# Later rope products and earlier up chunks in the score phase of a fused transformer layer

## The chip, the core and the metric

One core of one Trainium2 chip runs the whole layer in one launch. The metric is device microseconds of that core.

## The reference

The layer takes x of shape (4, 256, 256): 4 batches of 256 tokens, width 256.

```python
x = x + attn(layernorm(x)); x = x + ffn(layernorm(x))
# attn: q, k, v = h @ Wq.T, h @ Wk.T, h @ Wv.T ; rope over the full width on q and k
#   16 heads of 16; k_feat, q_feat = elu(k) + 1, elu(q) + 1
#   mem_out = (q_feat @ (k_feat.T @ v)) / (q_feat @ k_feat.sum)     # linear attention
#   attn = softmax(q @ k.T / 4) @ v
#   out = (g * mem_out + (1 - g) * attn) @ Wo.T,  g = sigmoid(gate) per head
# ffn: hidden = silu(x @ W1.T) * (x @ W3.T)     # 1024 wide
#   out = fwht(hidden) @ W2.T                   # Walsh-Hadamard transform, normalised
```

## The kernel before, in words

All engines are programmed by hand: each has its own list of instructions, run in order, and they meet at semaphores. Nothing is planned by a compiler, so the place of a call in an engine's list is its place in that engine's queue.

A product that needs full precision is made of three fp32r matmuls: each operand is split in a high part (rounded, written by ACT) and a low part (the rest, written by DVE or POOL). The Hadamard transform is multiplied into W2 at the start, in round 0.

The work runs in rounds. Round r holds the attention of batch r, the projections of batch r+1 and the feed-forward part of batch r-1, with the last chunk (7) of batch r-2. It has these phases:

- The score phase, heads h = 0 to 15. PE computes the scores of head h+2 (a pair of matmuls, L978) into one of two score banks; DVE reduces them to row maxima (L698), and PE can only write a bank again when DVE has read it. In the same loop PE does the residual and output projection of batch r-1 (L1056, L1065), the q and k projection of batch r+1 (`project_qk`), the transposes of the second LayerNorm's rows (L938), up unit 0 and 1 of chunk 7 of batch r-2 (at h = 5 and 6), the v projection of batch r+1 (`project_v`, at h = 8 and 9) and the up units of chunks 0 to 2 of batch r-1 (`UP_AT`, at h = 10 to 15). A chunk is 128 of the 1024 hidden columns; it has two up units (W1 and W3), each six matmuls (L1087, L1091). DVE does, beside the row maxima, the LayerNorm (`ln_statistics`, `ln_normalise` L681), the four rope products of batch r+1 (`rope_product` L709, at h = 3 to 6), `low_h2T` (L690, at h = 7) and the gates (`ffn_gate` L806, L809) of chunk 7 (h = 6) and chunk 0 (h = 12).
- The bridge. PE transposes the maxima (`transpose_max` L988), reads the linear memory (`read_memory` L1046), does chunk 3's up units and the down products (`ffn_down` L1109, L1113) of chunks 0 and 1. ACT (`split_max` L373) and DVE (`low_max`) write the negated maxima, and DMAs put them in rows of q_stack.
- The exp phase, heads 0 to 15. PE computes the shifted scores (`shifted_scores` L996), ACT takes their exponent (L384), and PE multiplies by v (`product_v` L1013); chunks 4 to 6 and the down products of chunks 2 to 6 lie in between.

The banks matter at three places. `project_v` of batches 1 to 3 writes misc_bank0, which batch r+1's second q and k projection (c = 1) has written before, so for batches 2 and 3 it waits for the fourth rope product; for batch 1 the q and k projections lie in exp banks. Chunk 2 uses the same bank as chunk 0 and waits for chunk 0's gate (`hid_s`). `read_memory` writes misc_bank0 again, so it waits for `evac_v` (L348).

ACT in the score phase: the second residual's copy (L398), tanh of chunk 7 (L413), h2T_hi (L404), the high parts of the roped q and k (`split_parts` L340, two), hid_hi of chunk 7 (`split_hid` L419), `evac_v`, then `ffn_step` of chunks 0 and 1, and `split_max`. `ffn_step(n)` is tanh of chunk n and hid_hi of chunk n-1.

POOL in a round: the reciprocal root of the LayerNorm (`ln_power` L551, called rstd below), two rope sums (L558), hid_lo of chunk 7 (`hid_low` L577), the low parts of the roped q and k (L565, two), in round 1 alone the low part of W2 (L617, tile w_lo), the negative part for elu (L569), hid_lo of chunks 0, 1 and the others. PE's down product of a chunk ends with matmuls on hid_lo (L1113). ACT's tanh of chunk n waits for hid_lo of chunk n-3.

SP loads the stacks of batch r+1: it waits for exp head 8 (or 16) of batch r, writes zeros, then copies part_hi and part_lo. Each wait is one in a fixed order.

Of the kernel before, what the change touches and what calls it, by code (L numbers as in the profile page):

```python
# [88 lines left out]
def build(nc, x, wqT, wkT, wvT, woT, gate, w1T, w3T, w2T, const, out):  # L89
    with ExitStack() as ctx:  # L90
# [112 lines left out]
        def chunk(b, c):  # L203

            return FC * b + c if 0 <= b < NB else None
# [17 lines left out]
        def has(b):  # L223
            return 0 <= b < NB
# [93 lines left out]
        def _(act):  # L318
# [81 lines left out]
            def evac_h2T(b):  # L400
                act.wait_ge(h2T_ps, b + 1)
                if b >= 1:
                    act.wait_ge(up_ps, FC * b)
                act.activation(h2T_hi[:], pv_bank[:], ACT.Copy).then_inc(h2T_hi_s, 1)  # L404
# [74 lines left out]
            for r in range(NB):  # L479
                if has(r - 1):  # L480
                    evac_x2(r - 1)
                if has(r - 2):
                    ffn_tanh(chunk(r - 2, 7))
                if has(r - 1):
                    evac_h2T(r - 1)
                if has(r + 1):
                    split_parts(r + 1, 0)
                if has(r - 2):
                    split_hid(chunk(r - 2, 7))
                if has(r + 1):  # L490
                    split_parts(r + 1, 1)
                if r >= 1 and has(r + 1):
                    evac_v(r + 1)
                ffn_step(chunk(r - 1, 0))
                ffn_step(chunk(r - 1, 1))
                if has(r):
                    split_max(r)
                ffn_step(chunk(r - 1, 2))
                if has(r):
                    evac_lin(r, 0)  # L500
                    evac_lin(r, 1)
                ffn_step(chunk(r - 1, 3))
                for h in range(NH):
                    if has(r):
                        exp_head(r, h)
                    if h in (2, 6, 12):
                        ffn_step(exp_chunk(r, {2: 4, 6: 5, 12: 6}[h]))
                    if h == 12 and r == NB - 1:
                        split_hid(chunk(r - 1, 5))
                    if h == 5 and has(r + 1):  # L510
                        exp_elu(r + 1)
                    if h == 8 and has(r + 2):
                        evac_hT(r + 2)
                    if h == 11 and has(r):
                        evac_att(r, 0)
                    if h == 15 and exp_chunk(r, 6) is not None:
                        split_hid(chunk(r - 1, 6))
                if has(r):
                    evac_att(r, 1)
                if has(r + 1):  # L520
                    evac_kfT(r + 1)
                if has(r):
                    evac_att(r, 2)
                if r == 0:
                    split_w2()
# [14 lines left out]
        def _(pool):  # L540
# [64 lines left out]
            for r in range(NB):  # L605
                if has(r - 1):
                    ln_power(LN[(2, r - 1)])
                if has(r + 1):
                    rope_sums(r + 1, 0)
                if has(r + 1):  # L610
                    rope_sums(r + 1, 1)
                hid_low(chunk(r - 2, 7))
                if has(r + 1):
                    low_parts(r + 1)
                if r == 1:
                    pool.wait_ge(w2_hi_s, 1)
                    pool.tensor_tensor(w2_lo[:], w2_b, w2_hi[:].bitcast(F32), ALU.subtract).then_inc(w2_lo_s, 1)  # L617
                if r == 0:
                    butterfly(pool, 0)
                    ln_power(LN[(1, 2)])  # L620
                if has(r + 1):
                    negative_part(r + 1)
                if r == 0:
                    butterfly(pool, 1)
                hid_low(chunk(r - 1, 0))
                hid_low(chunk(r - 1, 1))
                for c in range(2, FC - 1):
                    hid_low(exp_chunk(r, c))
                    if c == 3 and r > 0 and has(r + 2):
                        ln_power(LN[(1, r + 2)])  # L630
                    if c == 4 and has(r):
                        norm_linear(r)
# [8 lines left out]
        def _(dve):  # L641
# [205 lines left out]
            for r in range(NB):  # L847
                for h in range(NH):
                    if h == 0 and has(r - 1):
                        combine(r - 1, NP - 1)  # L850
                    if has(r) and h < NH - 2:
                        row_maxima(r, (h + 2,))
                    if h == 2 and has(r - 1):
                        ln_statistics(LN[(2, r - 1)])
                    if h == 12 and r == 0:
                        memory_strips(0)
                    if 3 <= h < 7 and has(r + 1):
                        rope_product(r + 1, h - 3)
                    if h == 3 and has(r - 1):
                        ln_normalise(LN[(2, r - 1)])  # L860
                    if h == 6:
                        ffn_gate(chunk(r - 2, 7))
                    if h == 7 and has(r - 1):
                        low_h2T(r - 1)
                    if h == 12:
                        ffn_gate(chunk(r - 1, 0))
                if r == 0:
                    ln_statistics(LN[(1, 2)])
                if has(r):
                    low_max(r)  # L870
                if r == 0:
                    gate_weights()
                ffn_gate(chunk(r - 1, 1))
                ffn_gate(chunk(r - 1, 2))
                if has(r - 2):
                    second_residual(r - 2)
                if r > 0 and has(r + 2):
                    ln_statistics(LN[(1, r + 2)])
                ffn_gate(chunk(r - 1, 3))
                if has(r + 2):  # L880
                    ln_normalise(LN[(1, r + 2)])
                ffn_gate(chunk(r - 1, 4))
                if has(r):
                    weights(r, 0)
                if has(r + 1):
                    features(r + 1)
                ffn_gate(chunk(r - 1, 5))
                if has(r + 2):
                    low_hT(r + 2)
                ffn_gate(exp_chunk(r, 6))  # L890
                if has(r):
                    combine(r, 0)
                if has(r + 1):
                    row_maxima(r + 1, (0,))
                if has(r):
                    combine(r, 1)
                if has(r + 1):
                    row_maxima(r + 1, (1,))
                    memory_strips(r + 1)
# [14 lines left out]
        def _(pe):  # L914
# [219 lines left out]
                free[bank.name] = (had_sb, u + 1)  # L1134


            UP_AT = ((),) * 10 + ((0,), (1,), (2,), (3,), (4,), (5,))

            UP_IN_EXP = {0: (4, 0), 1: (4, 1), 3: (5, 0), 4: (5, 1), 8: (6, 0), 11: (6, 1)}
            DOWN_IN_EXP = {2: 2, 7: 3, 12: 4}  # L1140
# [25 lines left out]
            for r in range(NB):  # L1166


                for h in range(NH):
                    if has(r) and h < NH - 2:  # L1170
                        scores(r, (h + 2,))
                    if h == 0 and has(r - 1):
                        residual_in(r - 1)
                    if h in (1, 2) and has(r - 1):
                        project_out(r - 1, h - 1)
                    if has(r + 1):
                        if h in (0, 1) or h in (2, 3) and r == 0:
                            project_qk(r + 1, h)
                        if h in (3, 4) and r >= 1:
                            project_qk(r + 1, h - 1)  # L1180
                    if r == 0 and h in (4, 5):
                        project_v(1, h - 4)
                    if r == 0 and h in (6, 7):
                        hadamard(2, h - 6, True)
                    if r == 0 and 8 <= h < 12:
                        hadamard(3, h % 2, h >= 10)
                    if h == 8 and r == 0:
                        transpose_features(0)
                    if h == 11 and r == 0:
                        memory(0)  # L1190
                    if h == 6 and has(r - 1):
                        transpose_rows(LN[(2, r - 1)])
                    if h in (5, 6):
                        ffn_up(chunk(r - 2, 7), h - 5)
                    if h in (8, 9) and r >= 1 and has(r + 1):
                        project_v(r + 1, h - 8)
                    if h == 9:
                        ffn_down(chunk(r - 2, 7))
                    for i in UP_AT[h]:
                        ffn_up(chunk(r - 1, i // 2), i % 2)  # L1200
# [84 lines left out]
```

## Time and profile before

| what | value |
|---|---|
| median of 3 runs | 217.6 us (216.65 to 218.44) |
| profiled execution | 218.47 us, span 216.7 us |
| granted TensorE clock | mean 0.976 |
| PE busy | 193.2 us (89%) |
| DVE busy | 148.2 us (68%) |
| ACT busy | 99.2 us (46%) |
| POOL busy | 92.0 us (42%) |

The span runs from the first to the last instruction of the profiled execution. Busy shares are means over all phases; the phases differ. In the rows of a timeline the times are the start and the duration, and the bracket tells how long the engine was idle before and what ended the wait. Rows of several equal instructions are merged ("x2"), their duration is then that of all of them. On PE two matmuls overlap, so one of 0.28 us is followed by the next after 0.12.

### The profile page before, as it was taken

How to read it: one execution, taken by the hardware profiler on the slowest of the kernel's cores; microseconds unless marked ns; L12 is line 12 of the kernel's file. 1: busy time of each engine (PE TensorE's matmuls, PEld its weight loads, DVE VectorE, ACT ScalarE, POOL GpSimd, SP SyncE). 2: the span in 40 equal slices, each digit the busy share in tenths (PEclk: the TensorE clock that was granted, in tenths of full speed). 3: DMA queues.
4: the chain of work that ended last, by engine and by line, in shares of the span. 5: the costliest groups of instructions: out<-in, count | busy, mean ns of one | idle time of the engine just before them, and what ended most of it. 6: DMA issues, size and time to landing. Idle time of an engine off the chain costs nothing.

```text
span 216.7 us, 4078 instructions
## 1 busy us (share of the span) xinstructions
PE 193.2 (89%) x1476; PEld 164.2 (76%) x1476; DVE 148.2 (68%) x329; ACT 99.2 (46%) x199; POOL 92.0 (42%) x84
## 2 busy tenths in 40 slices
PE   7898898499995998999979999996689988979993
PEld 3396797347794997878968998785589966869993
DVE  6499898963899963569898636299796345754442
ACT  3356715287722344884024368840215677231330
POOL 7719999990003895342039521320112231030332
PEclk9999999957999999999999999999999999997999
DMA  6998620003430000053100000533000100001001
GB/s 179 356 371 186 188 70 0 9 0 80 116 105 0 2 9 0 0 153 99 53 0 0 3 8 0 148 91 110 0 3 6 48 3 2 0 3 48 0 3 48
DMA packets 12639, 13.54 MB, mean 62 GB/s; under 512 B 1388, under 2 KB 11852, under 8 KB 12620
## 3 DMA queue, kind: packets, MB, share of 16 engines
q1 hardware_dynamic: 11148, 11.96, 18.6%
q10 hardware_dynamic: 1472, 1.32, 2.2%
q8 instruction: 12, 0.20, 0.4%
q14 instruction: 7, 0.06, 0.1%
HBM read 5.71 MB, written 1.05 MB: 31 GB/s over the span
## 4 chain that ended last, share of the span: by engine, by line
issue 38%; PE 27%; POOL 23%; DVE 7%; ACT 2%; POOLq 1%; DVEq 0%; ACTq 0%
PE exp_bank L1087 5%; POOL hid_lo L577 5%; PE score_bank L1144 4%; POOL w_lo L603 4%; PE score_bank L1087 3%; POOL prod L569 3%; PE exp_bank L1091 3%; PE down_bank L1109 2%; POOL narrow_raw L584 2%; POOL w_lo L596 2%; DVE prod L709 2%; POOL w_lo L617 2%; DVE rowmax_pad L698 2%; POOL part_lo L565 2%; PE score_bank L1091 2%
## 5 line engine op out<-in xcount | busy, mean ns | idle before, releaser
L577 POOL TENSOR_TENSOR hid_lo<-wide_raw,hid_hi 128x256 fp32r<-128x256 f32 x32 | 23.9, 747 | 71.4 <-ACT hid_hi L419 71.4
L698 DVE TENSOR_REDUCE rowmax_pad<-score_bank 128x2 f32<-128x512 f32 x64 | 42.8, 681 | 4.3 <-PE score_bank L978 4.2
L384 ACT ACTIVATE prob<-exp_bank 128x512 f32<-128x512 f32 x64 | 37.0, 601 | 17.2 <-PE exp_bank L996 16.7
L978 PE MATMUL score_bank<-k_stack,q_stack 128*128 128x256 f32 x128 | 27.3, 303 | 8.6 <-DVE rowmax_pad L698 8.5
L996 PE MATMUL exp_bank<-q_stack,k_stack 128*128 128x256 f32 x128 | 27.6, 318 | 4.1 <-DMA q_stack<-nmT_lo 2.3
L996 PEld LDWEIGHTS exp_bank<-q_stack,k_stack 128*128 128x128 f32 x128 | 19.9, 203 | 11.7 <-ACT prob L384 6.7
L978 PEld LDWEIGHTS score_bank<-k_stack,q_stack 128*128 128x128 f32 x128 | 19.3, 189 | 12.2 <-DVE rowmax_pad L698 8.3
L551 POOL TENSOR_TENSOR rstd<-var_eps,mhalf 128x2 f32<-128x2 f32 x8 | 5.6, 704 | 37.5 <-DVE var_eps L671 37.5
L806 DVE SCALAR_TENSOR_TENSOR wide_raw<-wide_raw,score_bank 128x256 f32<-128x256 f32 x16 | 6.7, 417 | 20.0 <-ACT wide_raw L413 20.0
L413 ACT ACTIVATE wide_raw<-exp_bank 128x256 f32<-128x256 f32 x16 | 6.1, 384 | 29.1 <-PE exp_bank L1091 27.1
L1087 PE MATMUL exp_bank<-h2T_hi,w_hi 128*128 128x256 f32 x64 | 17.8, 300 | 0.7 <-ACT h2T_hi L404 0.7
L1109 PE MATMUL down_bank<-w_hi,hid_hi 128*128 128x256 f32 x64 | 17.3, 293 | 0.0
L1087 PE MATMUL score_bank<-h2T_hi,w_hi 128*128 128x256 f32 x64 | 17.1, 291 | 0.0
L1087 PE MATMUL exp_bank<-h2T_hi,w_lo 128*128 128x256 f32 x64 | 16.9, 286 | 0.0
L1109 PE MATMUL down_bank<-w_lo,hid_hi 128*128 128x256 f32 x64 | 16.7, 283 | 0.0
L1087 PE MATMUL score_bank<-h2T_hi,w_lo 128*128 128x256 f32 x64 | 16.4, 280 | 0.0
L419 ACT ACTIVATE hid_hi<-wide_raw 128x256 fp32r<-128x256 f32 x32 | 13.3, 417 | 3.4 <-DVE wide_raw L809 3.1
L1113 PE MATMUL down_bank<-w_hi,hid_lo 128*128 128x256 f32 x64 | 13.1, 286 | 1.0 <-POOL hid_lo L577 0.9
L1013 PE MATMUL pv_bank<-prob,v_strips 128*32 128x256 f32 x192 | 13.7, 406 | 0.1
L1087 PEld LDWEIGHTS exp_bank<-h2T_hi,w_hi 128*128 128x128 f32 x64 | 12.6, 197 | 1.3 <-ACT h2T_hi L404 0.9
L1091 PE MATMUL exp_bank<-h2T_lo,w_hi 128*128 128x256 f32 x64 | 13.1, 286 | 0.0
L1087 PEld LDWEIGHTS exp_bank<-h2T_hi,w_lo 128*128 128x128 f32 x64 | 12.7, 198 | 0.0
(142 smaller groups left out, 483.2 us busy)
## 6 DMA issues: line engine op xcount, KB each, us to landing
q_stack<-part_hi SPq DMA_DIRECT2D x16, 128.0 KB
k_stack<-part_hi SPq DMA_DIRECT2D x14, 128.0 KB
xs<-in_x SPq DMA_DIRECT2D x4, 256.0 KB, 3.2
prob<-in_w2T SPq DMA_DIRECT2D x1, 1024.0 KB, 9.4
wide_raw<-in_w1T SPq DMA_DIRECT2D x1, 1024.0 KB, 11.4
wide_raw<-in_w3T SPq DMA_DIRECT2D x1, 1024.0 KB, 12.8
q_stack<-part_lo SPq DMA_DIRECT2D x8, 128.0 KB
k_stack<-part_lo SPq DMA_DIRECT2D x7, 128.0 KB
```

Source lines behind the costliest of these rows:

```text
L384: act.activation(prob[:, h % 8], exp_bank[h % 2][:], ACT.Exp, scale=SCALE).then_inc(prob_s, 1)
L419: act.activation(hid_hi[:, n % 3, :], ffn_work[n % 3], ACT.Copy).then_inc(hid_hi_s, 1)
L577: pool.tensor_tensor(hid_lo[:, n % 3, :], ffn_work[n % 3], hid_hi[:, n % 3, :].bitcast(F32), ALU.subtract).then_inc(hid_lo_s, 1)
L603: pool.tensor_tensor(w13_lo[:, m, k, cols], wide_raw[:, m, k, cols], w13_hi[:, m, k, cols].bitcast(F32), ALU.subtract).then_inc(done, 1)
L698: dve.tensor_reduce(rowmax[:, h, :], score_bank[h % 2][:], AX.X, ALU.max).then_inc(rowmax_s, 1)
L978: mm = pe.matmul(bank[:, tt, :], q_stack[:, h, tt * P:tt * P + P], k_stack[:, h, :], start=True, stop=True)
L996: mm = pe.matmul(bank[:, tt, :], k_stack[:, h, tt * P:tt * P + P], q_stack[:, h, :], start=True, stop=True)
L1013: mm = pe.matmul(bank[STRIP * j:STRIP * j + STRIP, half, :], v_strips[b % 2][:, tt, h, :], prob[:, h % 8, tt, :], start=(tt == 0), stop=(t ...
L1087: pe.matmul(bank[:, m, :], w[:, m, k, cols], h2T_hi[:, k, :], start=(k == 0 and w is w13_hi), stop=False)
L1091: mm = pe.matmul(bank[:, m, :], w13_hi[:, m, k, cols], h2T_lo[:, k, :], start=False, stop=(k == DC - 1))
L1109: pe.matmul(bank[:, tt, :], hid_hi[:, n % 3, tt * P:tt * P + P], w[:, c, :], start=(c == 0 and tt == 0 and w is w2_hi), stop=False, skip_g ...
L1113: mm = pe.matmul(bank[:, tt, :], hid_lo[:, n % 3, tt * P:tt * P + P], w2_hi[:, c, :], start=False, stop=(c == FC - 1), skip_group_check=True)
```

## The change

In rounds 1 and 2 the four rope products on DVE move from h = 3 to 6 to h = 8 to 11 (round 0 keeps 3 to 6). `low_h2T` moves from h = 7 to h = 6, ahead of row maximum 9. On PE, `UP_AT` brings up chunks 0 and 1 to h = 8 to 11 in rounds 1 to 3, and leaves chunk 2 at 14 and 15; the v projection of rounds 1 and 2 moves from h = 8 and 9 to h = 12 and 13. ACT's and POOL's lists follow: on ACT `ffn_step` of chunk 0 comes ahead of the two `split_parts`, that of chunk 1 between them and `evac_v`; on POOL the rope sums come behind hid_lo of chunk 7 and, in round 1, behind the low part of W2, and hid_lo of chunks 0 and 1 come around the low parts, ahead of the negative part.

```diff
--- before.py
+++ after.py
@@ -483,16 +483,15 @@
                     ffn_tanh(chunk(r - 2, 7))
                 if has(r - 1):
                     evac_h2T(r - 1)
+                if has(r - 2):
+                    split_hid(chunk(r - 2, 7))
+                ffn_step(chunk(r - 1, 0))
                 if has(r + 1):
                     split_parts(r + 1, 0)
-                if has(r - 2):
-                    split_hid(chunk(r - 2, 7))
-                if has(r + 1):
                     split_parts(r + 1, 1)
+                ffn_step(chunk(r - 1, 1))
                 if r >= 1 and has(r + 1):
                     evac_v(r + 1)
-                ffn_step(chunk(r - 1, 0))
-                ffn_step(chunk(r - 1, 1))
                 if has(r):
                     split_max(r)
                 ffn_step(chunk(r - 1, 2))
@@ -605,16 +604,17 @@
             for r in range(NB):
                 if has(r - 1):
                     ln_power(LN[(2, r - 1)])
-                if has(r + 1):
-                    rope_sums(r + 1, 0)
-                if has(r + 1):
-                    rope_sums(r + 1, 1)
                 hid_low(chunk(r - 2, 7))
-                if has(r + 1):
-                    low_parts(r + 1)
                 if r == 1:
                     pool.wait_ge(w2_hi_s, 1)
                     pool.tensor_tensor(w2_lo[:], w2_b, w2_hi[:].bitcast(F32), ALU.subtract).then_inc(w2_lo_s, 1)
+                if has(r + 1):
+                    rope_sums(r + 1, 0)
+                    rope_sums(r + 1, 1)
+                hid_low(chunk(r - 1, 0))
+                if has(r + 1):
+                    low_parts(r + 1)
+                hid_low(chunk(r - 1, 1))
                 if r == 0:
                     butterfly(pool, 0)
                     ln_power(LN[(1, 2)])
@@ -622,8 +622,6 @@
                     negative_part(r + 1)
                 if r == 0:
                     butterfly(pool, 1)
-                hid_low(chunk(r - 1, 0))
-                hid_low(chunk(r - 1, 1))
                 for c in range(2, FC - 1):
                     hid_low(exp_chunk(r, c))
                     if c == 3 and r > 0 and has(r + 2):
@@ -854,13 +852,14 @@
                         ln_statistics(LN[(2, r - 1)])
                     if h == 12 and r == 0:
                         memory_strips(0)
-                    if 3 <= h < 7 and has(r + 1):
-                        rope_product(r + 1, h - 3)
                     if h == 3 and has(r - 1):
                         ln_normalise(LN[(2, r - 1)])
+                    k = h - 3 if r == 0 else h - 8
+                    if 0 <= k < 4 and has(r + 1):
+                        rope_product(r + 1, k)
                     if h == 6:
                         ffn_gate(chunk(r - 2, 7))
-                    if h == 7 and has(r - 1):
+                    if h == 6 and has(r - 1):
                         low_h2T(r - 1)
                     if h == 12:
                         ffn_gate(chunk(r - 1, 0))
@@ -1134,7 +1133,7 @@
                 free[bank.name] = (had_sb, u + 1)
 
 
-            UP_AT = ((),) * 10 + ((0,), (1,), (2,), (3,), (4,), (5,))
+            UP_AT = ((),) * 8 + ((0,), (1,), (2,), (3,), (), (), (4,), (5,))
 
             UP_IN_EXP = {0: (4, 0), 1: (4, 1), 3: (5, 0), 4: (5, 1), 8: (6, 0), 11: (6, 1)}
             DOWN_IN_EXP = {2: 2, 7: 3, 12: 4}
@@ -1192,8 +1191,8 @@
                         transpose_rows(LN[(2, r - 1)])
                     if h in (5, 6):
                         ffn_up(chunk(r - 2, 7), h - 5)
-                    if h in (8, 9) and r >= 1 and has(r + 1):
-                        project_v(r + 1, h - 8)
+                    if h in (12, 13) and r >= 1 and has(r + 1):
+                        project_v(r + 1, h - 12)
                     if h == 9:
                         ffn_down(chunk(r - 2, 7))
                     for i in UP_AT[h]:
```

## Rows read from the trace of the kernel before

**Rows 1.** Busy time by stretch: us, PE, PEld, DVE, ACT, POOL, PEclk, DMA share, GB/s.
```profile
129.00:145.00 16.00, 16.00 (x160) 13.06 (x159) 9.05 (x21) 12.58 (x27) 4.07 (x5) 1.00 0.25 66
145.00:165.00 20.00, 15.62 (x111) 14.02 (x110) 16.26 (x38) 3.22 (x8) 2.20 (x3) 1.00 0.15 43
```

**Rows 2.** PE in order of time, round 1: start us, us, instruction, idle before.
```profile
68.11 0.47 PE L978 MATMUL score_bank<-k_stack,q_stack 128*128 128x256 f32 x2 [1.43 <-DVE rowmax_pad L698]
68.42 0.60 PE L938 MATMUL pv_bank<-cst,xn 128*128 128x128 f32 x4
...
78.22 0.27 PE L988 MATMUL pv_bank<-cst,rowmax_pad 128*128 128x128 f32 x1
...
82.95 0.50 PE L1113 MATMUL down_bank<-w_hi,hid_lo 128*128 128x256 f32 x2 [0.89 <-POOL hid_lo L577]
...
84.00 0.40 PE L996 MATMUL exp_bank<-q_stack,k_stack 128*128 128x256 f32 x2
```

**Rows 3.** DVE in order of time, round 1.
```profile
66.64 0.73 DVE L681 TENSOR_SCALAR xn<-xs,mv,rstd 128x256 f32<-128x256 f32 x2
...
69.67 0.68 DVE L698 TENSOR_REDUCE rowmax_pad<-score_bank 128x2 f32<-128x512 f32 x1
70.27 0.68 DVE L709 TENSOR_TENSOR prod<-misc_bank,cst 128x512 f32<-128x512 f32 x1
```

**Rows 4.** ACT in order of time, round 1.
```profile
69.06 0.60 ACT L404 ACTIVATE h2T_hi<-pv_bank 128x512 fp32r<-128x512 f32 x1 [3.32 <-PE pv_bank L938]
```

**Rows 5.** POOL in order of time, rounds 1 and 2.
```profile
65.61 0.72 POOL L551 TENSOR_TENSOR rstd<-var_eps,mhalf 128x2 f32<-128x2 f32 x1 [16.95 <-DVE var_eps L671]
...
71.12 1.30 POOL L558 TENSOR_TENSOR roped<-prod 128x512 f32<-128x512 f32 x1 [1.12 <-DVE prod L709]
...
74.87 4.59 POOL L617 TENSOR_TENSOR w_lo<-wide_raw,w_hi 128x2048 fp32r<-128x2048 f32 x1
79.43 2.78 POOL L569 TENSOR_SCALAR prod<-roped 128x1024 f32<-128x1024 f32 x1
...
108.80 0.69 POOL L551 TENSOR_TENSOR rstd<-var_eps,mhalf 128x2 f32<-128x2 f32 x1 [8.35 <-DVE var_eps L671]
```

**Rows 6.** PE in order of time, end of round 2's score phase, start of its exp phase.
```profile
122.67 0.27 PE L988 MATMUL pv_bank<-cst,rowmax_pad 128*128 128x128 f32 x1
...
127.51 0.40 PE L996 MATMUL exp_bank<-q_stack,k_stack 128*128 128x256 f32 x2
```

**Rows 7.** PE in order of time, round 3's score phase.
```profile
154.41 0.60 PE L938 MATMUL pv_bank<-cst,xn 128*128 128x128 f32 x4
154.76 0.36 PE L1087 MATMUL exp_bank<-h2T_hi,w_hi 128*128 128x256 f32 x1
...
157.71 0.50 PE L978 MATMUL score_bank<-k_stack,q_stack 128*128 128x256 f32 x2 [1.51 <-DVE rowmax_pad L698]
...
160.88 0.40 PE L978 MATMUL score_bank<-k_stack,q_stack 128*128 128x256 f32 x2
...
162.84 0.38 PE L1087 MATMUL exp_bank<-h2T_hi,w_hi 128*128 128x256 f32 x1
...
164.32 0.27 PE L988 MATMUL pv_bank<-cst,rowmax_pad 128*128 128x128 f32 x1
```

**Rows 8.** DVE in order of time, round 3's score phase.
```profile
156.17 0.42 DVE L806 SCALAR_TENSOR_TENSOR wide_raw<-wide_raw,exp_bank 128x256 f32<-128x256 f32 x1 [0.87 <-ACT wide_raw L413]
...
157.57 0.68 DVE L690 TENSOR_TENSOR h2T_lo<-pv_bank,h2T_hi 128x512 fp32r<-128x512 f32 x1
...
161.92 0.41 DVE L806 SCALAR_TENSOR_TENSOR wide_raw<-wide_raw,exp_bank 128x256 f32<-128x256 f32 x1
```

**Rows 9.** ACT in order of time, round 3: tanh of chunk 7.
```profile
155.76 0.38 ACT L413 ACTIVATE wide_raw<-exp_bank 128x256 f32<-128x256 f32 x1 [3.82 <-PE exp_bank L1091]
```

**Rows 10.** DVE in order of time, round 0: normalise beside POOL's negative part.
```profile
42.46 1.45 DVE L681 TENSOR_SCALAR xn<-xs,mv,rstd 128x256 f32<-128x256 f32 x2 [0.26 <-POOL rstd L551]
```

**Rows 11.** Busy time by stretch, round 0's exp phase.
```profile
46.00:48.00 2.00, 2.00 (x16) 1.09 (x18) 0.46 (x1) 1.71 (x4) 2.00 (x3) 0.50 0.00 0
```

## The prediction

> **What bounds the kernel now.** I read the busy time by stage first, then each engine's instructions in order of time. A round r has a score phase (sixteen heads, each a score pair on PE and a row maximum on DVE), a bridge (maxima transposed, memory read, feed-forward chunks) and an exp phase. In an exp phase PE is busy for 16.00 of 16.00 us; in the last score phase for 15.62 of 20.00 [rows 1]. So bridge and exp phases cost what PE has to do, and time is won or lost where PE waits: in the score phases, and once in a bridge.
>
> In the score phases PE waits for row maxima (1.43 us before a score pair of round 1 [rows 2], 1.51 us in round 3 [rows 7]), and DVE runs without a gap, one operation per 0.60 us: a row maximum at 69.67, the rope product behind it at 70.27 [rows 3]. So DVE's order sets the early part. The end is set by one wait: up chunk 2 shares its bank with chunk 0 and starts 0.92 us after chunk 0's gate starts (161.92 to 162.84 [rows 7, 8]); its two units take 1.48 us until the transpose of the maxima, 0.12 us a matmul, hence 0.72 for a unit of six and 0.24 for a score pair.
>
> The bridge takes 4.84 us in rounds 2 (122.67 to 127.51 [rows 6]) and 5.78 in round 1 (78.22 to 84.00 [rows 2]). The 0.94 more is PE waiting for hid_lo, 0.89 by its row: POOL came to it only at 82.2, after w2_lo (4.59) and the negative part (2.78) [rows 5].
>
> **The change part by part.** Round 0 keeps its order on every engine. Instructions and DMAs are the same in number. The stack loads on SP wait for exp heads and for part_lo; part_lo comes some 7 us later than now but still inside the bridge (about 82.2 in round 1, worked out below), well ahead of exp head 8, so SP loses nothing.
>
> *w2_lo on POOL, round 1.* It now starts straight after rstd, at 66.33 (65.61 + 0.72 [rows 5]), in a stretch where POOL waits for products anyway. That takes 4.59 us from in front of hid_lo and frees up to 0.94: **-0.94**.
>
> *Its neighbour.* LayerNorm's normalise on DVE waits for the same rstd, so it now starts beside w2_lo. The one normalise that started beside a long POOL operation took 1.45 us for its two instructions [rows 10] against 0.73 [rows 3]. I take **+0.72**; the lower end is 0. The Trainium skill (GPSIMD Engine Reference, the hardware table's line on SBUF interfaces) says that GpSimd contends with VectorE instructions in a two-port mode or with two SBUF inputs; by that rule alone both normalise instructions could be held, some +1.44. That trace agrees with a hold, but its 0.72 in all is what I use.
>
> *Rope products from heads 3-6 to 8-11, rounds 1 and 2.* DVE now uses products to fill the time in which LayerNorm, transposes and h2T come round. Without them it waits there, and the products come later with no gap between them. The new critical path, from the start of rstd:
>
> Round 1: rstd to normalise 0.78; normalise 0.65 (0.73 less the overlap of 0.08 that 0.68 long, 0.60 apart shows [rows 3]); row maximum 6 to score pair 8, 0.74 (in round 3, 156.97, one step before 157.57, to 157.71 [rows 7, 8]); to the transposes 0.31, to h2T_hi 0.64 (68.11, 68.42, 69.06 [rows 2, 4]); to low_h2T 0.63; low_h2T 0.60; then eight steps of 0.60 (maxima 9 to 13, three products) to the fourth product, 4.80. The v projection takes over the bank that the products read, so it starts 0.74 after that product's start (by the same hand-over); v 0.72, score pair 0.24, v 0.72, chunk 2 1.48. Sum 13.05; now 65.61 to 78.22 is 12.61 [rows 2, 5]: **+0.44**.
>
> Round 2 has the last chunk of the batch before in between: after the transposes come its second up unit (0.35), tanh (1.00), gate (0.41), 0.80 of gate before low_h2T [rows 7 to 9]. 0.78 + 0.65 + 0.74 + 0.31 + 0.35 + 1.00 + 0.41 + 0.80 + 0.60 + 4.80 + 0.74 + 0.72 + 0.24 + 0.72 + 1.48 = 14.34, against 13.87 now (108.80 to 122.67 [rows 5, 6]): **+0.47**. DVE waits some 1.0 us for tanh here, a wait that the products cover now.
>
> *Up chunks 0 and 1 two heads earlier, round 3.* No rope and no v here. low_h2T moves ahead of row maximum 9, so score pair 11 starts 0.60 later than 157.71. Chunk 0's gate stands behind row maximum 14 on DVE, and score pair 14 has one unit more in front of it: from pair 11 to pair 14 four units and three pairs, 3.60, where now 3 units and pairs, 2.88, take 3.17 with a short wait in them (157.71 to 160.88 [rows 7]). Pair 14 comes at 161.91: 1.03 late, or 1.32 if the 0.29 of waits stays. Gate and chunk 2 follow at their distances (1.04 and 0.92); nothing is left on PE for that time, since the units that covered it (1.96 from pair 14 to chunk 2) were moved ahead. **+1.03**, upper end +1.32. In rounds 1 and 2 the v projection fills that hole.
>
> *v projection and its evacuation.* On ACT the evacuation now stands behind both rope splits and in front of the split of the maxima. The fourth product starts 3.90 before the transpose of the maxima; rope sum 0.85 after it (70.27 to 71.12 [rows 3, 5]), 1.30 long; four small ACT operations, each no longer than the 0.60 of h2T_hi [rows 4] and overlapping by 0.1, end 0.85 + 1.30 + 2.0 = 4.15 after the product, just as the transposed maxima arrive: costs 0, at most 0.3 in each of two rounds.
>
> *POOL behind it.* hid_lo of chunk 0, two low parts (taken as long as a sum, 1.30), hid_lo of chunk 1 now come before the negative part. In round 1 (transpose at 79.38 with the terms above, product at 75.48) that gives some 82.9 for hid_lo(1), wanted at about 83.9; the negative part (2.78) and hid_lo(2) end near 86.4, wanted at 86.8 (exp phase from 84.2, then three score pairs, two up units and four matmuls, 2.64). So cost 0, cover 0.4; round 2 is alike.
>
> Sum: -0.94 + 0.72 + 0.44 + 0.47 + 1.03 = **+1.72 us**. The profiled execution took 218.47 (216.7 span, 1.77 around it), which gives 220.2; it lies 0.9 over the median of 217.6, and against the median the forecast is **219.3**. With the ends: 218.6 (no contention) to 220.3 (contention twice, 1.32 in round 3).
>
> **The rivals.**
> *Faster: PE's holes are filled.* Up units now stand ready early, and PE has holes to put them in. If DVE did not set the pace, the 1.43 and 1.51 us waits would be filled and POOL's 0.94 come on top: -3.9, 213.7. For it: the size of the holes. Against it: the units lie behind score pairs in PE's order, and those wait for DVE, which has no gap [rows 3]. It decides if chunk 0's gate in round 3 comes no later after its score phase's start than now.
> *A wash.* DVE's shifts are absorbed (for instance the v wait is shorter than 0.74, and normalise isn't held) and POOL's relief remains: -0.94 + 0.47 + 0.4, about 217.5.
> *POOL's cover is gone.* If ACT or POOL is 1 us later than estimated, hid_lo(2) is late by 0.6 at the third chunk's down product in rounds 1 and 2: +1.2 more, 220.5.
> *The clock falls.* The hole of 1.43 us on PE in round 1 grows to 1.8 (score pair 8 at 65.61 + 0.78 + 0.65 + 0.72 + 0.74 = 68.50 instead of 68.11), and round 3 gets one of 1.5 before chunk 2. TensorE was granted 0.50 (the level of 1.2 GHz) from 46 to 48 us [rows 11], in a stretch that follows a thin use of PE; now all three later score phases run at 1.00 with holes of 1.4 to 1.5. A fall for 3.5 to 7 us costs half of it: 221.1 to 222.8 with the terms above. The Trainium skill (TensorE: Matmul & The Clock Gate, Part 1) has the idle array drop to half rate and come back when busy; the rows of rounds 1 and 3 speak against it at this size of hole.
>
> **How the numbers follow.** Forecast 0.62, filled holes 0.10, a wash 0.12, POOL's cover 0.08, clock 0.08. A measurement of this kernel tells no less than about 1% (2.2 us) from no change. Faster by more than 1% (under 215.4) is most of the filled holes: 0.07. Slower by more (over 219.8) is the clock, POOL's cover and the upper third of the forecast, whose middle is only 0.5 below that line: 0.28. Same 0.65. The range reaches from 217.0 (a wash, less the scatter of half a microsecond) to 221.2 (upper end of the forecast with one further wait); outside are the filled holes and most of the clock case.
>
> **What would show it.** Bridge of round 1: 4.84, no wait for hid_lo. Normalise of round 1 at 1.45 for two. Score phase from rstd to the transpose: 13.8 in round 1, 14.3 in round 2. DVE idle for some 1.0 us before the last chunk's gate in round 2. In round 3 a PE wait of about 1.4 us before chunk 2. I am wrong if chunk 0's gate in round 3 isn't later, or if an exp phase gets a new wait.

## The result and the profile after

The changed kernel takes 222.82 us (222.56 to 223.51, 4 runs), the kernel before 218.02 beside it; the ratio is 1.023, interval 1.018 to 1.028. It is slower by 2.3%, not by 0.8%, and the range (217.0 to 221.2) ends below it. The profiled execution took 222.70 us, its span is 220.9.

Where the 4.2 us between the two spans lie shows when both traces are cut at the same events: start of rstd, transpose of the maxima, first shifted scores, last pair of the last down product. The stretches that are not listed (the bridges of rounds 2 and 3, the exp phases of rounds 1 and 2) differ by 0.06 us or less each.

| stretch | before | after | difference | forecast |
|---|---|---|---|---|
| round 1: rstd to transpose | 12.61 | 18.38 | +5.77 | +1.16 |
| round 1: bridge | 5.78 | 4.68 | -1.10 | -0.94 |
| round 2: rstd to transpose | 13.87 | 14.39 | +0.52 | +0.47 |
| round 3: rstd to transpose | 12.52 | 13.61 | +1.09 | +1.03 |
| round 3's first shifted scores to the last down product | 43.85 | 42.28 | -1.57 | 0 |
| start to round 1's rstd | 65.61 | 65.14 | -0.47 | 0 |

Three of the four stretches with a forecast came out within 0.16 us of it. The whole miss is in round 1's score phase; the end's -1.57 and the start's -0.47, which are no part of the change, hid a part of it.

DVE of the changed kernel, round 1, in order of time; these answer to [rows 3] and [rows 10]:

```profile
64.97 0.68 DVE L696 TENSOR_REDUCE rowmax_pad<-score_bank 128x2 f32<-128x512 f32 x1
65.95 4.84 DVE L679 TENSOR_SCALAR xn<-xs,mv,rstd 128x256 f32<-128x256 f32 x2 [0.30 <-issue]
70.72 1.28 DVE L696 TENSOR_REDUCE rowmax_pad<-score_bank 128x2 f32<-128x512 f32 x2
```

POOL beside it, answering to [rows 5]:

```profile
65.14 0.72 POOL L550 TENSOR_TENSOR rstd<-var_eps,mhalf 128x2 f32<-128x2 f32 x1 [16.82 <-DVE var_eps L669]
65.83 4.50 POOL L610 TENSOR_TENSOR w_lo<-wide_raw,w_hi 128x2048 fp32r<-128x2048 f32 x1
77.68 1.30 POOL L557 TENSOR_TENSOR roped<-prod 128x512 f32<-128x512 f32 x1 [7.36 <-DVE prod L707]
```

and PE, answering to [rows 2]:

```profile
65.70 0.50 PE L977 MATMUL score_bank<-k_stack,q_stack 128*128 128x256 f32 x2
71.54 0.77 PE L977 MATMUL score_bank<-k_stack,q_stack 128*128 128x256 f32 x2 [5.34 <-DVE rowmax_pad L696]
72.11 1.06 PE L937 MATMUL pv_bank<-cst,xn 128*128 128x128 f32 x4
...
83.52 0.27 PE L987 MATMUL pv_bank<-cst,rowmax_pad 128*128 128x128 f32 x1
```

What to see: the normalise took 4.84 us for its two instructions instead of 0.73. By the trace of L679 in this stretch its first half took 4.52 and its second 0.40; w_lo ends at 70.33, and the first half at 70.47. DVE counts as busy meanwhile, so no wait shows on it. PE stood still for 5.34 us and came back at half rate: a score pair of 0.77 where 0.47 is usual. The busy times by stretch (window, its length, then PE, PEld, DVE, ACT, POOL, granted clock, DMA share and GB/s) show the fall, which lasts for 6.8 us, from 71.0 to 77.8:

```profile
68.00:70.00 2.00, 0.00 (x0) 0.00 (x0) 2.00 (x1) 0.00 (x0) 2.00 (x1) 1.00 0.00 0
70.00:72.00 2.00, 0.46 (x2) 0.49 (x3) 2.00 (x4) 0.00 (x0) 0.33 (x1) 0.75 0.00 0
72.00:74.00 2.00, 2.00 (x10) 1.72 (x9) 0.86 (x2) 0.60 (x1) 0.00 (x0) 0.50 0.00 0
74.00:76.00 2.00, 1.97 (x10) 1.98 (x10) 2.00 (x4) 0.00 (x0) 0.00 (x0) 0.50 0.00 0
76.00:78.00 2.00, 2.00 (x12) 2.00 (x12) 1.67 (x4) 0.39 (x1) 0.32 (x1) 0.54 0.00 0
```

### The profile page after: what moved, and what is told of

The parts are those of the page before. It is cut to its first block, busy times and chain, and to the rows that moved or that the text cites. A ratio compares the mean times of both kernels' runs of the same rounds, so it can differ in the third digit from the quotient of the medians.

```text
span 220.9 us, 4078 instructions
## 1 busy us (share of the span) xinstructions
PE 193.5 (88%) x1476; PEld 165.2 (75%) x1476; DVE 152.2 (69%) x329; ACT 98.9 (45%) x199; POOL 91.9 (42%) x84
## 4 chain that ended last, share of the span: by engine, by line
issue 37%; PE 29%; POOL 18%; DVE 12%; ACT 2%; POOLq 1%; DVEq 0%; ACTq 0%
POOL hid_lo L576 5%; PE exp_bank L1086 5%; DVE rowmax_pad L696 4%; PE score_bank L1143 4%; PE score_bank L1086 3%; DVE xn L679 3%; POOL w_lo L595 3%; PE score_bank L977 3%; PE exp_bank L1090 2%; POOL narrow_raw L583 2%; PE down_bank L1108 2%; DVE prod L707 2%; POOL roped L557 2%; PE score_bank L1090 2%; POOL part_lo L564 2%
## 5 line engine op out<-in xcount | busy, mean ns | idle before, releaser
L977 PEld LDWEIGHTS score_bank<-k_stack,q_stack 128*128 128x128 f32 x128 | 20.3, 200 | 12.0 <-issue 6.9
L679 DVE TENSOR_SCALAR xn<-xs,mv,rstd 128x256 f32<-128x256 f32 x16 | 10.7, 711 | 7.8 <-POOL rstd L550 6.9
L557 POOL TENSOR_TENSOR roped<-prod 128x512 f32<-128x512 f32 x6 | 7.7, 1291 | 12.5 <-DVE prod L707 12.5
```

The source lines that it names most:

```text
L557: pool.tensor_tensor(roped[:, c], prod[:, 2 * c], prod[:, 2 * c + 1], (ALU.subtract, ALU.add)[c]).then_inc(rope_sum, 1)
L679: dve.tensor_scalar(xn[:, tt, :], xs[:, b, tt, :], mv[:, tt, 0:1], rstd[:, tt:tt + 1], ALU.subtract, ALU.mult).then_inc(ln_xn, 1)
L977: mm = pe.matmul(bank[:, tt, :], q_stack[:, h, tt * P:tt * P + P], k_stack[:, h, :], start=True, stop=True)
```

## The experiments

The theory after the result, *the hold*: DVE's normalise waits for the end of the POOL instruction beside it, PE waits behind DVE, and PE's clock falls. The rival: the late rope products and the late v projection cost more than forecast, and the hold lies in a time that is lost anyway. All kernels compute the whole reference except where it is said.

**a_wait: the change without the hold.**

```diff
                 if r == 1:
                     pool.wait_ge(w2_hi_s, 1)
+                    pool.wait_ge(ln_xn, TT * (LN[(2, 0)] + 1))
```

> The changed kernel, with one wait more: in round 1 POOL starts the low part of W2 only when the normalise of the second LayerNorm is done. Theory (the hold): POOL's one long two-input instruction keeps the normalise on DVE from going on until it ends, PE stands still behind it and its clock falls. Then the normalise takes 0.73 us for its two instructions again, the stretch from rstd to the transpose of the maxima in round 1 shrinks from 18.4 to about 13.1 us, no fall of the clock there, and the time is about 217.5 us, near the kernel before. Rival (the late products and the late v projection are what costs): the stretch stays above 16 us and the time above 221.

217.55 us (10 runs), ratio 0.999 (0.995 to 1.002). The normalise takes 0.73, the stretch 13.11:

```profile
65.66 0.73 DVE L680 TENSOR_SCALAR xn<-xs,mv,rstd 128x256 f32<-128x256 f32 x2 [0.31 <-issue]
```

POOL's w_lo starts at 66.54, 0.15 us behind the normalise, and is as long (4.57). So one wait takes away 5.3 us. The forecast's path for this stretch without contention was 13.05: the rival falls.

**b_w2lo: the hold without the change.** In the kernel before only L617 moves, with its wait, to straight behind `ln_power`.

> The kernel before, with this one part of the change: in round 1 POOL does the low part of W2 straight after rstd, ahead of the rope sums. Everything on DVE, PE and ACT keeps the order of before. The hold: the normalise begins beside it and takes 4 us or more, PE stands still, the clock falls to 0.5 for some us, and the time is 220 to 222 us. Rival (late products): DVE's order is the old one, so nothing is lost; POOL's relief of 0.9 us stays and the time is about 217.

219.82 us, ratio 1.012 (1.004 to 1.020). DVE's order is the old one, and the stretch takes 17.46 instead of 12.61:

```profile
64.79 0.68 DVE L709 TENSOR_TENSOR prod<-misc_bank,cst 128x512 f32<-128x512 f32 x1
65.39 4.63 DVE L681 TENSOR_SCALAR xn<-xs,mv,rstd 128x256 f32<-128x256 f32 x2
```

This one move costs 4.85 us there and gives 1.1 back in the bridge. The hold alone, without the later rope products, makes the kernel slower. The total of 219.82 lies just under the 220 to 222 that was expected.

**a_pieces: w_lo in four instructions.** The one instruction that they replace, and PE's wait for all four, are left out here.

```diff
+                    for k in range(4):
+                        two = slice(2 * k, 2 * k + 2)
+                        pool.tensor_tensor(w2_lo[:, two, :], w2_b[:, two, :], w2_hi[:, two, :].bitcast(F32),
+                                           ALU.subtract).then_inc(w2_lo_s, 1)
```

> The changed kernel, with the low part of W2 cut into four instructions of a quarter each (about 1.15 us each) at the same place on POOL. If DVE waits for the end of the POOL instruction that runs, each of the two halves of the normalise waits at most for one piece: 1.3 to 2.5 us for both, and the time is 218.5 to 220. If DVE is held as long as POOL has work of this kind at all, it is 4.8 us for both again and the time stays at 222.8.

220.47 us, ratio 1.014 (1.006 to 1.021). Both halves of the normalise are held, each for one piece (1.28 and 1.35 us), and then go on though POOL has pieces left. A row of this kind gives the shortest, median and longest duration in ns:

```profile
L682 DVE TENSOR_SCALAR xn<-xs,mv,rstd x2: 1284/1316/1349, 66.6 to 67.8; 128x256 f32<-128x256 f32 x2
```

```profile
66.50 5.03 POOL L612 TENSOR_TENSOR w_lo<-wide_raw,w_hi 128x512 fp32r<-128x512 f32 x4
```

So what holds is one instruction, to its end. The stretch takes 15.41 us, 2.30 more than in a_wait; the clock fell here too, for 3.4 us from 70 on. The time is 0.5 above the 218.5 to 220 that was expected. In the profiled execution round 0's score phase took 27.40 us, in all others 25.6 to 25.9; no part of this edit explains that.

**a_onein: another kind of instruction on POOL.** The subtraction is replaced by `tensor_scalar(w2_lo, w2_b, 0.0, None, mult)`, so this kernel leaves out the low part of W2.

> The changed kernel with the low part of W2 left out of the computation: at its place POOL writes the same tile with a multiplication by zero, one input instead of two, the same 2048 columns. In the kernel before, the one normalise that started beside such a one-input instruction of POOL took 1.13 us, though that instruction ran on for 2.8. If the kind of POOL's instruction decides (one input leaves DVE its way in), the first half of the normalise takes about 1.1 us and the stretch is near 14. If any long POOL instruction holds it to its end, it takes 4 to 5.5 us again.

The first half took 5.42 us beside an instruction of 5.39:

```profile
L679 DVE TENSOR_SCALAR xn<-xs,mv,rstd x2: 395/2906/5416, 66.7 to 72.1; 128x256 f32<-128x256 f32 x2
```

```profile
66.62 5.39 POOL L610 TENSOR_SCALAR w_lo<-wide_raw 128x2048 fp32r<-128x2048 f32 x1
```

POOL's kind does not decide. This is a single run, 225.15 us. Why the first half of the normalise of round 0 [rows 10] got away after 1.12 us, and the second took its usual 0.40, beside an instruction of 2.77 stays open; every trace has both rows so. The same POOL line did hold var_eps to its end in round 1 of the kernel before (shown below). One difference shows in the traces and was not tried: this normalise starts 0.05 to 0.07 us after POOL's instruction, the held ones 0.11 to 0.34 after it.

**a_filled: the clock's share.** In round 1, ahead of score pair 8, PE does matmuls that nobody reads:

```diff
+                    if r == 1 and h == 6:
+                        bank = claim(exp_bank[0])
+                        for _ in range(20):
+                            pe.matmul(bank[:], wqkv_hi[:, 0, 0, 0:P], w13_hi[:, 0, 0, 0:512], start=True, stop=True)
```

> The changed kernel, with 20 matmuls of 512 columns more on PE (their product is never used), in round 1 ahead of score pair 8, where PE stands still for 5.3 us. The hold on DVE stays at 4.8 us. If the fall of the clock after that hole costs something of its own, the granted clock stays at 1.00 from 70 to 78 us and the stretch from rstd to the transpose shrinks from 18.4 to about 17.2 us, the time to 221.6. If DVE alone sets the pace there, the stretch stays at 18.4.

222.44 us (221.41 to 222.90), ratio 1.022 (1.013 to 1.030); the total is not told from the changed kernel's 222.82, the stretch is. The normalise takes 4.96 us, the clock stays at 1.00 in this stretch, and the stretch takes 17.41 instead of 18.38:

```profile
66.51 4.74 PE L1172 MATMUL exp_bank<-w_hi,wqkv_hi 128*128 128x512 f32 x20
72.12 0.47 PE L977 MATMUL score_bank<-k_stack,q_stack 128*128 128x256 f32 x2 [0.88 <-DVE rowmax_pad L696]
```

So of the 5.27 us between a_wait (13.11) and the changed kernel, 0.97 is the clock and 4.30 the hold, by one trace each. DVE sets most of the pace behind the hole: were PE the bound all through, half rate for 6.8 us would have cost 3.4.

**b_neg, b_r3, a_wait_r3: the other terms one by one.** b_neg moves `negative_part(r + 1)` on POOL behind `hid_low(chunk(r - 1, 1))` in the kernel before. b_r3 gives the kernel before the changed `UP_AT` and `low_h2T` at h = 6 in round 3 alone; a_wait_r3 takes these back in a_wait.

> The kernel before, with this one part of the change: on POOL the negative part stands behind hid_lo of chunks 0 and 1 instead of ahead of them (in round 0, where there are no chunks, nothing moves). Theory: POOL's lateness is all of the 0.94 us by which round 1's bridge is longer than the others, so the bridge takes 4.84 us instead of 5.78, no other stretch changes, and the time is 0.9 below the kernel before (ratio 0.996). Rival: hid_lo of chunk 2 is now late behind the negative part and the exp phase gives it back; ratio 1.000.

217.35 us, ratio 0.998 (0.994 to 1.002). Round 1's bridge takes 4.59 instead of 5.78, the other stretches of rounds 1 to 3 up to the last exp phase change by 0.05 or less, but the total is not told from no change. (This profile, of a run of 215.92, has no fall of the clock at the end and is 1.54 shorter there.)

> The kernel before, with the change in round 3 alone: up chunks 0 and 1 two heads earlier, low_h2T ahead of row maximum 9. Theory (the forecast's term): chunk 0's gate comes about 1.05 us later and PE waits for it before chunk 2; the stretch from rstd to the transpose in round 3 grows from 12.52 to 13.6 us, ratio 1.005. Rival (up units ahead of their time fill PE's holes): the stretch is 12.5 or less, ratio 1.000 or less.

218.33 us, ratio 1.003 (0.999 to 1.006), so the total is not told from no change here either. Round 3's stretch takes 13.64 instead of 12.52, as forecast. In this profile the clock fell in round 1, where nothing was changed: that stretch took 14.03 instead of 12.61.

> The changed kernel with POOL's wait for the normalise in round 1 (as in the run a_wait) and round 3 back in the order of before. If the terms add up, round 3's stretch is 12.5 us, and against a_wait's 217.55 the time falls by 1.05 to about 216.5, ratio to before 0.994; rounds 1 and 2 keep 13.1 and 14.4. If they don't add up (round 3's order was only hiding something later), it stays at 217.5.

217.71 us, ratio 0.999 (0.994 to 1.004), a miss. Round 3's stretch took 13.89, not 12.5. PE's order and its hole of 1.51 us are those of before, but now the clock fell behind the hole:

```profile
156.71 0.50 PE L978 MATMUL score_bank<-k_stack,q_stack 128*128 128x256 f32 x2 [1.51 <-DVE rowmax_pad L697]
```

```profile
155.00:157.00 2.00, 0.49 (x4) 0.30 (x3) 1.79 (x4) 1.05 (x3) 0.42 (x1) 1.00 0.00 0
157.00:159.00 2.00, 2.00 (x15) 1.81 (x15) 2.00 (x4) 0.00 (x0) 0.32 (x1) 0.87 0.00 0
159.00:161.00 2.00, 2.00 (x11) 2.00 (x11) 0.83 (x2) 0.00 (x0) 0.00 (x0) 0.50 0.03 8
```

Round 3 in one order, with the same hole, ran at full rate in the trace of before and fell to half rate in this one, at a price of about 1.4 us. The kernel before scatters by 3 us (216.2 to 219.4 over 25 runs), its mean granted clock lies anywhere from 0.965 to 0.976, and that hides terms of 1 us. How much of the scatter such falls make, the next runs show.

**b_clock, a_clock, b_best: the clock held.** PE gets such matmuls wherever it waits:

```diff
+            def fill(bank, count):
+                for _ in range(count):
+                    pe.matmul(claim(bank)[:], wqkv_hi[:, 0, 0, 0:P], wqkv_hi[:, 0, :, :].rearrange("p c n -> p (c n)"), start=True, stop=True)
+            FILL = {(1, 6): 5, (2, 6): 3, (3, 5): 4, (3, 9): 5}
...
+                if r == 0:
+                    fill(score_bank[0], 9)
...
+                    fill(misc_bank[0] if r == 3 else exp_bank[0], FILL.get((r, h), 0))
...
+            fill(score_bank[1], 3)
             transpose_rows(LN[(2, NB - 1)])
+            fill(score_bank[1], 3)
```

> The kernel before, with matmuls of 512 columns more on PE whose product is never used, at places where PE waits: 9 in round 0's bridge, 5 and 3 ahead of score pair 8 in rounds 1 and 2, 4 and 5 ahead of pairs 7 and 11 in round 3, and 3 and 3 around the last transposes. The traces so far show the granted clock at 0.5 for some 6 us in round 0's exp phase every time, and for 3 to 4 us in round 1, in round 3 or at the end in some executions and not in others of the same order. If these falls cost time of their own, the clock stays near 1.00, the time is 1.5 to 3 us under that of before, and its runs lie within about 1 us instead of 3. If PE isn't the bound where they fall, the time is that of before.

214.36 us, ratio 0.986 (0.982 to 0.989), its six runs 213.89 to 215.24 (before, beside it, 17 runs: 215.84 to 219.19). It is 3.5 below the kernel before, more than the 1.5 to 3 that was expected. Round 0's exp phase up to round 1's rstd takes 20.57 us instead of 22.64, and the stretch that answers to [rows 11] shows 1.00:

```profile
45.00:47.00 2.00, 2.00 (x23) 1.28 (x24) 0.64 (x1) 1.98 (x4) 2.00 (x3) 1.00 0.00 0
```

> The changed kernel with POOL's wait for the normalise (as in the run a_wait), and with matmuls more as in b_clock (3 ahead of pair 11 and 4 ahead of up chunk 2 in round 3). With the clock held on both sides this shows what the reordering without the hold costs: the terms 0.50, 0.50 and 1.05 of the three score phases less 1.05 of the bridge give 1.0 us over b_clock, ratio about 1.005 to it. If the later rope products cost nothing in the end, it equals b_clock.

215.81 us (215.38 to 216.71, 12 runs), 1.45 over b_clock, ratio of the medians 1.007. The stretches of rounds 1 to 3 are +0.51, +0.52 and +1.37 against b_clock (13.13, 14.38 and 13.88 where b_clock has 12.62, 13.86 and 12.51), the bridge -1.07: 1.33. Expected was 1.0 over b_clock, and round 3 makes the difference: it is 0.3 more than in the changed kernel; the four extra matmuls ahead of chunk 2 are the likely reason, which was not tried.

> As b_clock, with the negative part behind hid_lo of chunks 0 and 1 on POOL (as in the run b_neg), and in round 3 the gate of the last chunk behind row maximum 9 on DVE, where it now waits 0.87 us for tanh (1 matmul more ahead of pair 11 instead of 5). With the clock held the scatter is gone and the 0.94 us of round 1's bridge and some 0.25 of round 3 show: 1.2 us under b_clock, round 1's bridge 4.8 us, round 3's stretch from rstd to the transpose 12.3. If the scatter hid nothing, it equals b_clock.

213.76 us (213.07 to 214.06), ratio 0.982 (0.979 to 0.986), the fastest kernel here by the medians, 0.6 below b_clock, half of the 1.2 that was expected; the ranges of the two overlap. The bridge takes 4.58, 1.18 less than in b_clock. Yet the two profiled spans are equal (212.3 and 212.2), because in this execution the start was slower: round 1's rstd came at 63.70 instead of 62.67. Round 3 was a miss, 12.66 instead of 12.3: with the gate later, the down product ahead of score pair 12 now waits for hid_hi:

```profile
154.91 0.39 PE L1109 MATMUL down_bank<-w_hi,hid_hi 128*128 128x256 f32 x1 [0.72 <-ACT hid_hi L419]
```

## Why the prediction was wrong

*w2_lo on POOL, -0.94: right.* The bridge lost 1.10 in the changed kernel and 1.19 in b_neg. Either move was enough for it: the place of the negative part alone gives 1.19 (b_neg), that of w2_lo alone 1.12 (b_w2lo). So the move that brought the hold was not needed.

*Its neighbour, +0.72: the step that failed.* It measured +4.30, and with the clock 5.27 (the normalise itself went from 0.73 to 4.84). The mechanism, a hold beside a long POOL instruction, was named; its size was taken from the one row of the same instruction [rows 10]. The prediction treated the hold as a fixed price. It is what is left of POOL's instruction, and the trace of before showed that on other instructions. A tensor_scalar as small as var_eps and gsum takes 0.17 us when nothing holds it, ginv_lin 0.19:

```profile
79.43 2.78 POOL L569 TENSOR_SCALAR prod<-roped 128x1024 f32<-128x1024 f32 x1
81.62 0.60 DVE L671 TENSOR_SCALAR var_eps<-mv 128x2 f32<-128x2 f32 x1
```

```profile
39.28 2.49 POOL L252 TENSOR_TENSOR wide_raw<-att 128x512 f32<-128x512 f32 x2
39.41 1.15 DVE L671 TENSOR_SCALAR var_eps<-mv 128x2 f32<-128x2 f32 x1
40.68 1.11 DVE L819 TENSOR_SCALAR gsum<-gexp 128x4 f32<-128x4 f32 x1
```

```profile
45.15 2.50 POOL L252 TENSOR_TENSOR wide_raw<-wide_raw 128x512 f32<-128x512 f32 x2
45.49 0.98 DVE L773 TENSOR_TENSOR ginv_lin<-inv,gate 128x32 f32<-128x32 f32 x1
```

81.62 + 0.60 is 82.22, and POOL's instruction ends at 82.21. 39.41 + 1.15 is 40.56, the end of the first of two POOL instructions of 1.25, and the next ends with gsum. ginv_lin ends at 46.47, the first of its two POOL instructions at 46.42. Four rows said "to the end". [rows 10] did not, and neither did a tensor_scalar of 0.17 on gate (at 42.04) beside rstd; the prediction used [rows 10] alone. The upper end should have been the length of w_lo, 4.59, less the 0.1 that DVE starts later and the 0.4 that the half takes anyway: some 4.1. The Trainium skill (GPSIMD Engine Reference, Specifications, the line on SBUF interfaces) names two kinds of VectorE instructions that contend with GpSimd: those in a two-port mode and those with two SBUF inputs. The traces fit it in this: what was held is either a tensor_scalar from SBUF to SBUF (normalise, var_eps, gsum) or has two SBUF inputs (ginv_lin), while the row maxima (from PSUM) kept their 0.65 to 0.69 and low_h2T (one input from PSUM) its 0.68 to 0.69 beside POOL's instructions in all runs. No trace shows the mode of an instruction. The 1.44 that the prediction worked out for that rule was the same wrong row taken twice.

*Rope products in rounds 1 and 2, +0.44 and +0.47: right.* 13.11 in a_wait against the forecast 13.05, 14.39 against 14.34. One detail was wrong: DVE waits 0.87 us for tanh in round 2, not 1.0.

*Up chunks in round 3, +1.03: right.* +1.09, and +1.12 in b_r3. PE waits 1.23 us for chunk 0's gate, where about 1.4 was said:

```profile
168.57 0.39 PE L1086 MATMUL exp_bank<-h2T_hi,w_hi 128*128 128x256 f32 x1 [1.23 <-DVE wide_raw L807]
```

*v's evacuation and POOL's cover, 0: right.* No exp phase changed (24.80 and 24.30 us up to the next rstd in both kernels).

*The rivals.* The clock rival happened, though behind a hole of 5.3 us and not of 1.8: without the hold (a_wait) that hole is 1.23, and no fall follows. That the time lies at the upper end of this rival's 221.1 to 222.8 is luck: its price was a fall at PE's bound, the 0.97 measured here is less, and the hold makes up the rest. Its counter-argument, that holes of 1.4 to 1.5 us leave the clock alone, holds for the trace of before, but not for b_r3 (a fall behind 1.43 us) and a_wait_r3 (behind 1.51). Filled holes, the wash and POOL's cover did not occur.

*The end, -1.57.* The profile of before has a fall of the clock around the last transposes (0.50 from 194.5 to 198 us); that of the changed kernel and those of all experiments have none there, whatever their order in rounds 1 to 3. So it is taken for the same scatter, no effect of the change; that the kernel before always has it was not excluded by a second trace.

Put right, the sum is -1.10 + 5.77 + 0.52 + 1.09 = +6.3 from the stretches of the change. The end's -1.57 and the start's -0.47 bring it to the 4.2 between the two spans; between the medians it is 4.8. Which falls of the clock the other runs of either kernel had, no trace shows.

## What to carry to other kernels

Before a long POOL instruction is moved into a stretch where POOL is idle, list the short DVE instructions on SBUF that run beside it: each can be held until the POOL instruction ends, shows as busy and not as waiting, and PE stands still behind it. A wait on POOL for those instructions took the whole hold away here (POOL stood idle for 0.97 us instead); cutting the long instruction in four left 2.3 us of the 5.3. Where a measurement scatters by more than the effect looked for, look at the granted clock by stretch first: a few matmuls in PE's holes took 1.4% off this kernel, and its six runs lie within 1.35 us instead of 3.35. What is left has another source at least in part: the start, up to the second rstd (12.82 in the kernel before), took 11.6 to 13.05 us in the thirteen traces, and no edit touches it.

## What the runs showed of the hardware

- A normalise instruction of 0.41 us took 4.52 us beside a POOL instruction of 4.50, 5.42 beside one of 5.39, and 1.28 and 1.35 beside pieces of 1.26. A POOL instruction with one input holds it to the end as one with two does. The exception is the normalise of round 0, 1.12 us beside a POOL instruction of 2.77 in every trace, which stays open.
- The granted clock fell behind a hole of 1.51 us in round 3 of a_wait_r3 and not in round 3 of the kernel before, which has the same order there. A fall cost 0.97 us in round 1 behind the hold (against a_filled), 1.42 in round 1 of b_r3, 1.37 in round 3 of a_wait_r3 and 2.07 in round 0's exp phase (against b_clock).
- With the holes filled, the mean granted clock is 0.997 to 1.000 in all runs of b_clock, a_clock and b_best, against 0.965 to 0.976 before.
